# A fused delta-rule and feed-forward block: the chunk inverse is multiplied into masked products and keys, and the dense matmuls between the small ones are dealt out anew

## Time and profile before

| what | us |
|---|---|
| median of 3 runs | 2215.24 (2213.98 to 2216.39) |
| the profiled execution, its own time | 2216.21 |
| its span in the profile | 2214.5 |
| busy: PE, DVE, ACT, POOL | 2112.6, 1862.5, 1189.1, 285.4 |

### The profile page before, as it was taken

How to read it: one execution, slowest core, us unless ns; L and a number is a source line. 1 busy time by engine, 2 the same in 40 slices (tenths; PEclk the granted TensorE clock), 3 DMA queues, 4 the chain that set the end, 5 groups by cost and what they waited for, 6 DMA issues and landing times.

```text
span 2214.5 us, 87086 instructions
## 1 busy us (share of the span) xinstructions
PE 2112.6 (95%) x36976; PEld 1079.5 (49%) x36976; DVE 1862.5 (84%) x3348; ACT 1189.1 (54%) x3080; POOL 285.4 (13%) x534
## 2 busy tenths in 40 slices
PE   2789999999999999999999999999999999999996
PEld 1345454554545555454554545455454554545453
DVE  8887978889798887979888797888979888797886
ACT  4774545636456464645646455463645647455542
POOL 2101111021110201011020110201111020111100
PEclk9899999999999999999999999999999999999998
DMA  7001110001111011111001111001111001111000
GB/s 271 2 21 22 39 23 31 20 14 40 22 40 22 3 40 22 39 23 40 13 13 40 22 40 23 12 31 22 40 22 40 17 8 40 22 40 22 15 9 20
DMA packets 89971, 68.77 MB, mean 31 GB/s; under 512 B 68480, under 2 KB 68480, under 8 KB 89600
## 3 DMA queue, kind: packets, MB, share of 16 engines
q1 hardware_dynamic: 88880, 63.20, 10.4%
q10 hardware_dynamic: 720, 0.03, 0.0%
HBM read 30.72 MB, written 16.78 MB: 21 GB/s over the span
## 4 chain that ended last, share of the span: by engine, by line
PE 85%; DVE 7%; ACT 4%; issue 2%; DMA 1%; SPq 0%; ACTq 0%
PE D L478 27%; PE D L458 22%; PE D L547 13%; PE T L383 12%; PE D L399 8%; PE T L375 4%; DVE state L1412 2%; ACT kpv L781 1%; ACT at L807 1%; ACT f_hi L768 1%; DVE outer_p L1408 1%; DVE kpv L1397 1%; DMA qt<-in_L_attn_Wq_dram 1%; DVE outer_v L1298 0%; DVE at L1305 0%
## 5 line engine op out<-in xcount | busy, mean ns | idle before, releaser
L478 PE MATMUL D<-xt,wgu 128*128 128x512 f16 x3072 | 687.0, 381 | 9.1 <-issue 7.9
L458 PE MATMUL D<-xt,w_hi 128*128 128x512 f16 x1536 | 461.7, 383 | 23.9 <-DVE w_lo L1075 23.9
L478 PEld LDWEIGHTS D<-xt,wgu 128*128 128x128 f16 x3072 | 293.0, 98 | 360.3 <-issue 13.5
L458 PE MATMUL D<-xt,w_lo 128*128 128x512 f16 x768 | 293.5, 382 | 0.0
L547 PE MATMUL D<-wd,f_lo 128*128 128x512 bf16 x768 | 292.7, 381 | 0.0
L547 PE MATMUL D<-wd,f_hi 128*128 128x512 bf16 x768 | 292.2, 381 | 0.0
L863 ACT ACTIVATE qt<-T 64x128 f32<-64x128 f32 (+1 forms) x384 | 104.7, 273 | 348.5 <-DVE outer_p L1408 345.5
L1298 DVE TENSOR_TENSOR outer_v<-mt,at 128x62 f32<-128x62 f32 (+15 forms) x496 | 259.5, 523 | 13.6
L1305 DVE TENSOR_TENSOR at<-at,outer_v 128x62 f32<-128x62 f32 (+15 forms) x496 | 260.4, 525 | 11.8
L764 ACT ACTIVATE kpv<-kpv,rk 128x32 f32<-128x32 f32 x1024 | 231.2, 308 | 33.8 <-DVE kpv L1167 33.8
L458 PEld LDWEIGHTS D<-xt,w_hi 128*128 128x128 f16 x1536 | 145.6, 98 | 196.8 <-issue 28.8
(11 more groups left out here) (182 smaller groups left out, 2928.3 us busy)
## 6 DMA issues: line engine op xcount, KB each, us to landing
xs<-_attn_hidden_states_dram SPq DMA_DIRECT2D x32, 512.0 KB, 3.6
out_dram<-xs SPq DMA_DIRECT2D x32, 512.0 KB, 2.8
fuse<-in_L_ffn_gate_w_dram SPq DMA_DIRECT2D x2, 768.0 KB, 8.4
xs<-in_L_ffn_up_w_dram SPq DMA_DIRECT2D x2, 768.0 KB, 9.0
f_hi<-in_L_ffn_down_w_dram SPq DMA_DIRECT2D x2, 768.0 KB, 10.6
f_lo<-in_L_ffn_down_w_dram SPq DMA_DIRECT2D x2, 768.0 KB, 12.2
kpv<-in_L_attn_Wk_dram SPq DMA_DIRECT2D x1, 1024.0 KB, 11.2
qt<-in_L_attn_Wq_dram SPq DMA_DIRECT2D x1, 1024.0 KB, 13.4
```

The source lines that it names most:

```text
L458: last = nc.tensor.matmul(D[bank][:, :], w[:, k, cols], xp[:, k, :], start=n == 0, stop=n == len(products) - 1)
L478: last = nc.tensor.matmul(D[bank][:, :], wgu[:, n // 2, c:c + P], (xt_hi, xt_lo)[n % 2][:, n // 2, :], start=n == 0, stop=n == 2 * KT_ - 1)
```

## The change

PE now multiplies the transposed inverse by the masked products and the keys, `kpv[:, 0:2]` in place of `kpv[:, 1:3]`. With `P' = P Tinv` and `K' = K Tinv` (each in its turned form) the chain works on plain keys and values: `r = v - k S` in part A, and part B multiplies `r` by `P'` and `K'`. The sums are the same ones in another grouping.

- `t_transposed` reads `t_prob` by columns (elements 32 apart) in place of reading it in one run.
- `read_w` is gone: `kq` keeps the keys. ACT's `copy_products` takes both halves of each group from PSUM to `kpv`, 512 elements a partition where `copy_u` took 256, and waits for PE itself.
- Semaphores `u_ready` and `w_ready` become `pk_ready`. The inverse stage no longer waits for the values (`vk_ready`); DVE's first subtraction does. The first `pairs` wait for six groups, the first `quads` for all eight.
- `FILL_UW` goes from 10 to 12 and `FILL_CHAIN` from (6, 7) to (6, 6). The total stays at 144 dense matmuls a turn.
- ACT: `norm_rows` and `high_part` stand at other places between the copies. In the first turn `beta_tanh` comes after the third group of queries. DVE: `low_part` 9 comes before the chain, 10 and 11 and `fuse_tile(11)` at other places of its first two steps.

```diff
-FILL_UW, FILL_CHAIN = 10, (6, 7)
+FILL_UW, FILL_CHAIN = 12, (6, 6)
...
-                    pe.wait_ge(vk_ready, since(1, 1))
...
-                            pe.wait_ge(u_ready, since(8, 2 * m - 2))
+                            pe.wait_ge(pk_ready, since(8, 2 * m - 2))
...
-                                             kpv[:, 1:3, pc * DH:(pc + 1) * DH], b == 1)
+                                             kpv[:, 0:2, pc * DH:(pc + 1) * DH], b == 1)
...
-                        if c == 0:
-                            pe.wait_ge(w_ready, since(8, 8))
...
-                        pe.wait_ge(*((o_ready, since(STEPS, c - 1)) if c >= 2 else (u_ready, since(8, 8))))
+                        pe.wait_ge(*((o_ready, since(STEPS, c - 1)) if c >= 2 else (pk_ready, since(8, 6 + 2 * c))))
...
+                        if c == 0:
+                            pe.wait_ge(pk_ready, since(8, 8))
                         pe.wait_ge(r_ready, since(STEPS, c + 1))
...
-                    def copy_u(g):
-                        act.wait_ge(w_ready, since(8, g + 1))
-                        made = T[g % 4][:, :].rearrange("p (n a d) -> p n a d", n=8, a=2)
+                    def copy_products(g):
+                        act.wait_ge(tiled_done, since(TILED, DONE_UW + g + 1))
+                        made = T[g % 4][:, :].rearrange("p (n a d) -> p a n d", n=8, a=2)
                         for to, src in parts_of(g % 2):
-                            last = nc.scalar.activation(vt[to, 8 * g:8 * g + 8, :], made[src, :, 1, :], ACT.Copy)
-                        last.then_inc(u_ready, 1)
+                            last = nc.scalar.activation(kpv[to, 0:2, 8 * g * DH:8 * (g + 1) * DH].rearrange("p a (n d) -> p a n d", n=8),
+                                                        made[src], ACT.Copy)
+                        last.then_inc(pk_ready, 1)
...
-                        nc.vector.transpose(tt[:, s], t_prob[:, s]).then_inc(tt_ready, 1)
-
-                    def read_w(g):
-
-                        dve.wait_ge(tiled_done, since(TILED, DONE_UW + g + 1))
-                        nc.vector.transpose(kq[:, 8 * g:8 * g + 8, 0, :],
-                                            T[g % 4][:, :].rearrange("p (n a d) -> p n a d", n=8, a=2)[:, :, 0, :]).then_inc(w_ready, 1)
+                        nc.vector.transpose(tt[:, s], t_prob[:, s].rearrange("p i c -> p c i")).then_inc(tt_ready, 1)
```

More of the change, by code:

```diff
@@ L215, in delta_block_kernel @@
         q_sqs = [fuse[:, 2, :], fuse[:, 3, :], sg[:, 0, :], sg[:, 1, :]]
-        u_v = vt[:, :, :].rearrange("p (m b c) d -> p b c m d", m=MS, b=BATCH)
+        r_v = vt[:, :, :].rearrange("p (m b c) d -> p b c m d", m=MS, b=BATCH)
         ot_v = qt[:, :, :].rearrange("p (m b c) t -> p b c m t", m=MS, b=BATCH)
@@ L270, in delta_block_kernel @@
         tt_ready, p_ready = sem("tt_ready"), sem("p_ready")
-        u_ready, w_ready, r_ready, s_ready = sem("u_ready"), sem("w_ready"), sem("r_ready"), sem("s_ready")
+        pk_ready, r_ready, s_ready = sem("pk_ready"), sem("r_ready"), sem("s_ready")
         ws_read, ds_read = sem("ws_read"), sem("ds_read")
@@ L728, in all_spans @@
                         magnitude_of(GU_PIECES + 1)
-                        beta_tanh()
                         square_of(2)
@@ L734, in all_spans @@
                         evacuate_q(2)
+                        beta_tanh()
                         square_of(5)
@@ L830, in all_spans @@
                     scaled.then_inc(vk_ready, 1)
-                    copy_u(0)
-                    copy_u(1)
+                    norm_rows(0)
+                    copy_products(0)
+                    copy_products(1)
+                    norm_rows(1)
                     silu_gate(9)
-                    norm_rows(0)
-                    copy_u(2)
-                    copy_u(3)
+                    copy_products(2)
+                    copy_products(3)
+                    high_part(8)
+                    norm_rows(2)
                     silu_gate(10)
-                    high_part(8)
-                    norm_rows(1)
-                    copy_u(4)
-                    copy_u(5)
+                    copy_products(4)
+                    copy_products(5)
+                    norm_rows(3)
                     high_part(9)
-                    norm_rows(2)
-                    copy_u(6)
-                    copy_u(7)
+                    copy_products(6)
+                    copy_products(7)
                     silu_gate(11)
-                    norm_rows(3)
+                    high_part(10)
                     if not opening:
@@ L853, in all_spans @@
                             square_q(SQUARE_AT[c])
-                        if c < 2:
-                            high_part(10 + c)
+                        if c == 1:
+                            high_part(11)
                         if c in HIGH_AT and not closing:
@@ L1354, in all_spans @@
                     t_transposed(1)
-                    read_w(0)
                     low_part(0)
-                    read_w(1)
                     low_part(1)
                     low_part(2)
-                    read_w(2)
                     low_part(3)
-                    read_w(3)
                     fuse_tile(8)
@@ L1365, in all_spans @@
                     low_part(5)
-                    read_w(4)
                     low_part(6)
-                    read_w(5)
                     fuse_tile(9)
                     low_part(7)
-                    read_w(6)
                     low_part(8)
-                    read_w(7)
                     fuse_tile(10)
+                    low_part(9)
                     def read_down(j):
@@ L1393, in all_spans @@
                         if c == 0:
-                            dve.wait_ge(u_ready, since(8, 8))
+                            dve.wait_ge(vk_ready, since(1, 1))
                         dve.wait_ge(ws_read, since(STEPS, c + 1))
-                        u = u_v[:, :, c]
-                        nc.vector.tensor_tensor(u, u, blocks(outer_v), ALU.subtract).then_inc(r_ready, 1)
+                        r = r_v[:, :, c]
+                        nc.vector.tensor_tensor(r, r, blocks(outer_v), ALU.subtract).then_inc(r_ready, 1)
                         if c:
                             add_inner(c - 1)
-                        if c < 2:
-                            low_part(9 + c)
+                        if c == 0:
+                            fuse_tile(11)
+                        if c == 1:
+                            low_part(11)
                         if c in DOWN_FIRST:
@@ L1415, in all_spans @@
                         if c == 0:
-                            fuse_tile(11)
-                        if c == 1:
-                            low_part(11)
+                            low_part(10)
                         if c in LOW_AT:
```

## The result

| | before | the change |
|---|---|---|
| median, us | 2214.72 (2213.98 to 2216.39, 4 runs) | 2230.65 (2229.26 to 2235.11, 4 runs) |
| profiled execution, us | 2216.21 | 2229.26 |
| its span, us | 2214.5 | 2227.6 |
| granted TensorE clock, mean | 0.992 | 0.986 |

The ratio is 1.0073, with a 95% interval of 1.0060 to 1.0085: the change is slower by 0.7%. The forecast for it was 2234.1.

What follows compares the result with a forecast made beforehand. It took PE's work as the bound, with part B's loop through DVE even with it at 2.40 us. 2216.2 + 13.5 (dense matmuls) + 5.4 (transpose) = 2235.1, less 1.0 gives 2234.1 us; range 2225 to 2247.

Steps and rivals of the forecast that it cites:

- Part B is even with its loop: Part B of a chain step: the loop `quads`, `outer_p`, state, `pairs` takes 2.40 us, PE's own work the same.
- The waits foretold at 0.2 and 0.55: PE's waits for the state in part B: about 0.2 us in all seven hand-overs, 0.55 in the two with slow state.
- Dense matmuls in the inverse, +1.73 - 0.68: Inverse stage: eight more dense matmuls add 1.73 us a turn, the stall of 0.68 before the chain goes; +1.05.
- Behind the last step, -0.22: End of the chain: no `pairs` wait there, so one dense matmul less saves 0.22 us a turn.
- The transpose: Inverse read by columns on DVE: 2.05 us each, PE waits 0.34 a turn, +5.4 us in sixteen turns.
- The free transpose (0.25): Rival on DVE's turned inverse: reading by columns costs nothing, total 2228.7 us; chance 0.25.
- ACT's copies: Twelve longer copies a turn on ACT, +2.6 us of its time, expected to be hidden from PE: nothing taken.
- The walk: ACT's order followed copy by copy: room of 1.6 us before batch three and 2.7 before the first `quads`.
- the missing `read_w`: DVE's eight transposes, 3.6 us a turn, go from the inverse stage, where DVE waits for PE anyway: nothing gained.
- the rival of 0.05: ACT's copies, queued behind `norm_rows`, hold batch three or the first `quads`: +10.8 us, 2244.9; chance 0.05.
- The first turn: Opening turn: moving `beta_tanh` frees PE from a 5.80 us wait, but DVE's solve sets the time: nothing gained.
- the sum: Whole kernel: 2216.2 + 13.5 for dense matmuls + 5.4 for the column read, less 1.0: median 2234.1 us, 0.85% slower.

Runs made afterwards that it cites:

- the second profile of the change: The change itself, unaltered, measured once more beside other runs: 2232.18 us, ratio 1.0079 to the kernel before.
- the old split and the copies first: The change with 10 and (6, 7) dense matmuls and ACT's first two product copies ahead of the first `norm_rows`: 2214.96 us, ratio 0.9990.
- the shifted run with the old split: The change with 10 and (6, 7) dense matmuls, `HALF_SLOT` 114 for 94, and ACT's order close to the kernel before: 2221.16 us, ratio 1.0026.

## Why the prediction came out right

- **Part B is even with its loop: right.** It is 2.40 to 2.41 with seven, six and five. The waits foretold at 0.2 and 0.55 are 0.15 and 0.55 in the timeline, 5 x 0.15 + 2 x 0.55 = 1.85 a turn, 29.6 us in sixteen. The list has 23.6, since it names the state in 73 of the 112 cases; the distances from start to start are the surer sign.
- **Dense matmuls in the inverse, +1.73 - 0.68: right.** Measured 16.86 - 15.81 = 1.05 a turn.
- **Behind the last step, -0.22: right** (0.20: from the last `quads` to the next turn's first small batch 13.60 became 13.40).
- **The transpose: mechanism right, size too large.** Estimated 2.05 us, measured 1.95; PE waits 0.23 in place of 0.34, so 3.7 us for 5.4. The row with single elements 128 bytes apart was the right one to price it by: (1950 - 1224) / 1024 = 0.71 ns an element, where it gave 0.8. The free transpose (0.25) falls, and so does, for this read of SBUF, the rule of "VectorE: DVE Perf Modes" in the Trainium skill; its "SBUF — State Buffer" spoke rightly against the change.
- **ACT's copies: "I take nothing" was nearly right, for a reason that was too narrow.** The walk took POOL's statistics as they fell in one turn. The prediction priced the missing `read_w` at "Nothing". With them gone DVE's `low_part` run in a row; in some turns POOL's operation beside them takes 3.29 us, which no turn of the kernel before has, and the third batch is 0.9 us late in two turns of the second profile of the change, in none of the first. With ten in place of twelve behind each batch the same costs 1.7 us in four turns of sixteen: the rival of 0.05 is true there, and twelve hide most of it. Missing gaps and the longer transposes go together there; which turns are hit is open.
- **The first turn: right.** PE's wait fell from 5.80 to 2.9 us and bought nothing: the first batch of the inverse starts at 145.33 in place of 144.77, 0.23 of it the transpose's.
- **The step that failed is the sum's silence on what the old places of the instructions cost.** Counted over the two profiles of the first comparison, part A of steps 5 and 6 holds 6.6 us above 2.03 in the kernel before and 3.2 in the change, of which part B of step 5 gives back 0.3 and 0.2. Part B of step 2 holds 1.1 and 0; it stands in all six profiles with seven dense matmuls there, shifted or not, and in none of the others; its cause is open. Together the change has 4.3 us less of these. So 18.9 - 1.7 (transpose) - 4.3 = 12.9; the spans differ by 13.1.
- **Part of the nearness is luck.** That account holds for this pair of profiles. The medians differ by 15.9 us, and by 16.9 when the change was measured again; in the profile of that run the same parts A hold 6.4 us, as much as in the kernel before, and two late third batches add 1.8. How near 15.9 and 16.9 came to the 18.9 forecast depends on how often these two fell, and the sum had a term for neither.

## What to carry to other kernels

Where the state of a recurrence goes round through another engine, compare the loop with the bottleneck engine's own work in it before moving work: when both are even, a list of waits shows next to nothing, and work taken out gives a wait in its place, while work put elsewhere is paid in full. An operation that is removed may have been the gap that let a third engine in (here it takes a later start of the row as well), so ask what its idle time did for others, and what each queue holds behind a wait that may now be late. Before a difference of under one per cent is explained by its edits, look for batches of equal instructions that differ in length; if they do, shift the code by a few slots and measure the noise that this alone makes.

## What the runs showed of the hardware that I had not expected

- Instructions have an address, and it costs: a batch of 32 small matmul records takes 0.83 to 0.97 us in place of 0.69 where a border of 256 slots lies in it, and some take up to 0.76 us more. The breaks stand at fixed records: with the old split and the copies first, counted from the second batch of the inverse, behind records 78, 205 and 333; in the shifted run with the old split behind 68, 195 and 323. They are 127 or 128 records apart, each with a weight load, and move by ten records when the code moves by 20 slots. Moving it took 7 us (0.3%) off the kernel before. Not each border costs: one 28 slots into the `pairs` of step 6 does in most turns, one at 30 does not, and the unshifted change pays at step 5 in seven of sixteen turns of one profile and in twelve of another, where the kernel before pays in fifteen. What decides this is open. The Trainium skill, "Runtime: NRT & Kernel Launch", section "Instruction fetch mechanics", has blocks of 256 instructions and calls the cost of crossing "mostly hidden"; here it is not, in batches of small matmuls.
- A VectorE transpose that reads SBUF at a step of 128 bytes takes 1950 ns where the one in a run takes 1224.
- Beside the same four `low_part` in a row, POOL's 128 x 4 operation takes 1.46 us in most turns and 3.29 in one of seven. VectorE's state takes up to 887 ns in place of 482 beside POOL's addition. The second costs a whole 1.05 us a turn, 18 us of the kernel: more than anything that the change touched.
